# Attention output turned by a DMA in f16 halves and projected in three f16 products

## The reference, cut to what matters

```python
def _L0_xattn_ref(queries, keys, values, attn_bias, Wq, Wk, Wv, Wp):
    q = _split_heads(queries @ Wq.T, N_HEAD, D_KEY)
    k = _split_heads(keys @ Wk.T, N_HEAD, D_KEY)
    v = _split_heads(values @ Wv.T, N_HEAD, D_VALUE)
    scores = jnp.einsum('bhqd,bhkd->bhqk', q, k) * D_MODEL ** (-0.5) + attn_bias
    weights = jax.nn.softmax(scores, axis=-1)
    out = jnp.einsum('bhqk,bhkd->bhqd', weights, v)
    ...
    return out @ Wp.T

x = x + _L0_xattn_ref(_layernorm(x), ctx_1024, ctx_1024, bias, Wq, Wk, Wv, Wp)
x = x + _L0_ffn_ref(_layernorm(x), ...)   # 8 experts, each takes its top tokens
```

## Time and profile before

| What | Value |
|---|---|
| median of the runs | 1128.0 us |
| the profiled execution's own time | 1129.07 us |
| its span | 1127.3 us |
| PE busy | 1066.8 us, 95% |
| DVE busy | 888.7 us, 79% |
| ACT busy | 810.8 us, 72% |
| POOL busy | 683.3 us, 61% |
| attention stage | to about 791 us of the span |

### The profile page before, as it was taken

The page is one execution under the profiler, slowest core; times in us unless marked ns, Lnnn a source line. Parts: engine busy times, 40 slices in busy tenths (PEclk is TensorE's granted clock), DMA queues, the critical chain, the costliest instruction groups (busy, mean ns, idle before and its releaser), DMA issues. The chain is left out here.

```text
span 1127.3 us, 46562 instructions
## 1 busy us (share of the span) xinstructions
PE 1066.8 (95%) x13640; PEld 868.2 (77%) x13640; DVE 888.7 (79%) x3847; ACT 810.8 (72%) x2407; POOL 683.3 (61%) x1155
## 2 busy tenths in 40 slices
PE   4999999999999999999999999998499999999995
PEld 3888888888888888888888888886256666666664
DVE  4898898898988988989989889887765656565553
ACT  4777778777877787787778777875366666667562
POOL 5566566565665665655656656654047767767673
PEclk9999999999999999999999999999589999999998
DMA  3765555555555555555555555555001121111112
GB/s 102 121 106 109 109 100 114 105 106 111 106 103 114 100 109 107 101 114 106 105 112 105 104 113 100 111 102 86 0 11 29 29 58 37 37 56 29 50 54 66
DMA packets 307337, 96.83 MB, mean 86 GB/s; under 512 B 284256, under 2 KB 300640, under 8 KB 307296
## 3 DMA queue, kind: packets, MB, share of 16 engines
q1 hardware_dynamic: 306432, 94.16, 41.7%
q10 hardware_dynamic: 864, 2.16, 0.5%
HBM read 16.58 MB, written 4.19 MB: 18 GB/s over the span
## 5 line engine op out<-in xcount | busy, mean ns | idle before, releaser
L408 ACT ACTIVATE probs<-neg,negmax 128x120 f32<-128x120 f32 x1024 | 320.3, 383 | 157.7 <-DVE negmax L430 157.6
L430 DVE CUSTOM_DVE_ANT_0 neg<-bk_s,bias_sb 128x120 f32<-128x120 f32 x1024 | 227.5, 277 | 77.3 <-PE bk_s L550 73.7
L270 POOL CAST p_parts<-probs 128x480 f16<-128x480 f32 x256 | 150.2, 587 | 135.6 <-ACT probs L408 131.8
L1098 POOL TENSOR_TENSOR hid<-hid_f,hid 128x512 f16<-128x512 f32 x128 | 167.7, 1314 | 73.9 <-ACT hid L1052 72.9
L550 PE MATMUL bk_s<-qk 64*128 64x120 f32 x2048 | 181.4, 296 | 0.5 <-DVE negmax L430 0.5
L498 DVE TENSOR_TENSOR p_parts<-probs,p_parts 128x480 f16<-128x480 f32 x256 | 177.6, 694 | 0.7 <-POOL p_parts L270 0.5
L550 PEld LDWEIGHTS bk_s<-qk 64*128 64x128 f32 x2048 | 134.2, 186 | 45.4 <-issue 45.3
L589 PE MATMUL bk_y<-wp_sb,oT 128*128 128x128 f32 x1024 | 156.3, 275 | 0.0
L1152 DVE TENSOR_TENSOR hid_f<-bk_u,silu 128x512 f32<-128x512 f32 x128 | 88.3, 690 | 85.3 <-ACT silu L1045 35.0
L378 ACT COPY qk<-bk_a 128x496 f32<-128x496 f32 x256 | 144.7, 565 | 3.3 <-PE bk_a L537 3.3
L589 PEld LDWEIGHTS bk_y<-wp_sb,oT 128*128 128x128 f32 x1024 | 134.5, 191 | 0.2 <-ACT oT L371 0.2
(11 more groups left out here) (161 smaller groups left out, 3399.9 us busy)
## 6 DMA issues: line engine op xcount, KB each, us to landing
y_all<-y SPq DMA_DIRECT2D x128, 64.0 KB, 2.0
wst<-ffn_w SPq DMA_DIRECT2D x64, 96.0 KB, 2.3
x_sb<-x SPq DMA_DIRECT2D x64, 64.0 KB, 2.0
pT<-p_parts SPq DMA_TRANSPOSE x256, 3.1
out<-x_sb SPq DMA_DIRECT2D x16, 256.0 KB, 2.0
ctx_f<-ctx_t SPq DMA_DIRECT2D x64, 60.0 KB, 1.9
w_f<-wqkv_t ACTq DMA_DIRECT2D x3, 512.0 KB, 5.4
wp_sb<-wp_t ACTq DMA_DIRECT2D x1, 512.0 KB, 6.2
```

The costliest lines, as they stand in the source:

```text
L270: pool.tensor_copy(p_parts[g][:, 0, :, 0:K], probs[g % 2][:, :, :]).then_inc(p_hi_ready, 1)
L408: e = nc.scalar.activation(probs[g % 2][:, i, :], neg[g % 2][:, i, :], ACT.Exp, bias=negmax[g % 2][:, i:i + 1], scale=-1.0)
L430: r = nc.vector.tensor_tensor_reduce(out=neg[g % 2][:, i, :], in0=bk_s[i % 2][:, (i // 2) * K:(i // 2 + 1) * K], in1=bias_sb[:, :], scale= ...
L1098: nc.gpsimd.tensor_tensor(hid[1][par][:, ic, :], hid_f[ic % 2][:, :], hid[0][par][:, ic, :], ALU.subtract).then_inc(hid_lo_ready, 1)
```

## The change

1. PE no longer turns O. ACT writes the upper f16 half of `o_sb` (`o_parts`), POOL the lower half, and SP issues a second DMA transpose per group, 128 x 512 f16, into `oT`, right behind the turn of the probabilities in its list (`turn_o(t, g)`: group n-5, behind `turn` of group n).
2. The projection reads `oT` and `wp_hi`, `wp_lo` (made once, times 16) in six f16 products per group in place of two f32 ones. It is now for group n-8 (`PROJ_LAG` 8, before 6), and stands before PV in PE's step.
3. V has two PSUM banks (the bank of `bk_x` is free), and V stands before projection and PV, Q and K come last.
4. In DVE's step `rsum` now stands ahead of `v_lo`; the addition of the projection to x moves from step 1 to step 3 of the slot; POOL's and ACT's lists are moved to fit. `pT` and `oT` lie in the space of `w_f`.

```diff
-TURN_LAG = PV_LAG + 1
-PROJ_LAG = PV_LAG + 2
+SPLIT_LAG = PV_LAG + 1
+PROJ_LAG = PV_LAG + 4
+X1_GROUP = (PROJ_LAG + 3) % 4
...
+        pT = [turned(2 * GH * i, 2 * GH) for i in range(GROUPS)]
+        oT = [turned(2 * GH * GROUPS + 2 * GP * i, 2 * GP) for i in range(GROUPS)]
+        o_parts = [sb(f"o_parts{i}", [S, 2, GH, DH], F16) for i in range(GROUPS)]
...
-        bk_a, bk_b, bk_o, bk_x, bk_y, bk_m = (bank(n) for n in ("bk_a", "bk_b", "bk_o", "bk_x", "bk_y", "bk_m"))
+        bk_b = [bank("bk_b0"), bank("bk_b1")]
+        bk_a, bk_o, bk_y, bk_m = (bank(n) for n in ("bk_a", "bk_o", "bk_y", "bk_m"))
...
+            def turn_o(t, g):
+                b5, g5 = behind(t, g, SPLIT_LAG)
+                if live(b5):
+                    n = 4 * b5 + g5
+                    sp.wait_ge(o_lo_ready, n + 1)
+                    alone(sp)
+                    if some(n - GROUPS + 1):
+                        sp.wait_ge(proj_written, n - GROUPS + 1)
+                    alone(sp)
+                    sp.dma_start_transpose(oT[g5][:, :, :], o_parts[g5][:, :, :, :].rearrange("p a b c -> p (a b c)")
+                                           ).then_inc(oT_moved[g5], 16)
             def slot(t, par):
...
+                for g in range(GROUPS):
+                    if live(t - 1):
+                        turn(t, g)
+                    turn_o(t, g)
+                    if g == 0 and live(t + 2):
+                        load_x(t + 2, par)
+                    if g == 1 and live(t + 1):
+                        load_ffn(t + 1, (par + 1) % 2)
...
+            def lower_o(t, g):
+                b5, g5 = behind(t, g, SPLIT_LAG)
+                if live(b5):
+                    pool.wait_ge(o_hi_ready, n + 1)
+                    pool.tensor_tensor(o_parts[g5][:, 1, :, :], o_sb[g5 % 2][:, :, :], o_parts[g5][:, 0, :, :],
+                                       ALU.subtract).then_inc(o_lo_ready, 1)
...
-                    act.wait_ge(oT_written, 4 * b4 + g4 + 1)
-                    nc.scalar.copy(oT[g4 % 2][:, :, :].rearrange("p a b -> p (a b)"),
-                                   bk_x[:, 0:GP * S]).then_inc(oT_ready, 1)
+                    act.wait_ge(o_ready, 4 * b5 + g5 + 1)
+                    nc.scalar.copy(o_parts[g5][:, 0, :, :], o_sb[g5 % 2][:, :, :]).then_inc(o_hi_ready, 1)
...
-                    for j in range(GP):
-                        m = nc.tensor.transpose(bk_x[:, j * S:(j + 1) * S],
-                                                o_sb[g3 % 2][:, 2 * j:2 * j + 2, :].rearrange("p a b -> p (a b)"),
-                                                ident[:, :])
...
-                        m = nc.tensor.matmul(bk_y[:, 0:D], oT[g4 % 2][:, j, :], wp_sb[:, GP * g4 + j, :],
-                                             start=(g4 == 0 and j == 0), stop=(g4 == GROUPS - 1 and j == GP - 1))
+                    pe.wait_ge(oT_moved[g4], 16 * (b4 + 1))
+                    for j in range(GP):
+                        at = GP * g4 + j
+                        oh, ol = oT[g4][:, j, :], oT[g4][:, GP + j, :]
+                        nc.tensor.matmul(bk_y[:, 0:D], oh, wp_hi[:, at, :], start=(g4 == 0 and j == 0), stop=False)
+                        nc.tensor.matmul(bk_y[:, 0:D], oh, wp_lo[:, at, :], start=False, stop=False)
+                        m = nc.tensor.matmul(bk_y[:, 0:D], ol, wp_hi[:, at, :], start=False,
+                                             stop=(g4 == GROUPS - 1 and j == GP - 1))
```

More of the change, by code:

```diff
@@ L378, in step @@
                     nc.scalar.copy(qk[pw][:, gw, :], bk_a[:, 0:QK]).then_inc(qk_ready, 1)
[L380 to L384, removed]
+                b5, g5 = behind(t, g, SPLIT_LAG)
+                if live(b5):
+                    act.wait_ge(o_ready, 4 * b5 + g5 + 1)
+                    if some(b5):
+                        act.wait_ge(oT_moved[g5], 16 * b5)
+                    alone(act)
+                    nc.scalar.copy(o_parts[g5][:, 0, :, :], o_sb[g5 % 2][:, :, :]).then_inc(o_hi_ready, 1)
                 if gw == 2:
@@ L422, in step @@
                 tw, gw, pw = (t, g - 1, par) if g else (t - 1, GROUPS - 1, (par + 1) % 2)
+                if g == 0 and live(t + 1):
+                    dve.wait_ge(loaded_xc, (t + 2) * 32)
+                    if some(t + 1):
+                        dve.wait_ge(stats_ready, t + 1)
+                    alone(dve)
+                    nc.vector.bn_stats(stats[:, 0, :], x_sb[:, t + 1, :]).then_inc(x_stats_ready, 1)
                 if live(t - 1):
@@ L461, in step @@
-                if live(b2):
-                    dve.wait_ge(rsum_ready, 4 * b2 + g2 + 1)
-                    if some(4 * b2 + g2 - 1):
-                        dve.wait_ge(oT_written, 4 * b2 + g2 - 1)
-                    nc.vector.scalar_tensor_tensor(
-                        out=o_sb[g2 % 2][:, :, :], in0=o[:, :, 0:DH], scalar=1.0 / WSCALE,
-                        in1=rsum[:, :].rearrange("p (a b) -> p a b", b=1).to_broadcast([S, GH, DH]),
-                        op0=ALU.mult, op1=ALU.mult).then_inc(o_ready, 1)
@@ new lines, in step @@
+                if g == X1_GROUP and live(t - 3):
+                    dve.wait_ge(proj_written, 4 * (t - 3) + 4)
+                    nc.vector.scalar_tensor_tensor(
+                        out=x_sb[:, t - 3, :], in0=bk_y[:, 0:D], scalar=1.0 / (WSCALE * WSCALE),
+                        in1=x_sb[:, t - 3, :], op0=ALU.mult, op1=ALU.add).then_inc(x1_ready, 1)
+                b4, g4 = behind(t, g, PV_LAG)
+                o = bk_o[:, 0:GH * OW].rearrange("p (a b) -> p a b", a=GH)
+                if live(b4):
+                    dve.wait_ge(pv_written, 4 * b4 + g4 + 1)
+                    if some(4 * b4 + g4):
+                        dve.wait_ge(o_ready, 4 * b4 + g4)
+                    nc.vector.reciprocal(rsum[:, :], o[:, :, DH]).then_inc(rsum_ready, 1)
@@ new lines, in step @@
+                if live(tw):
+                    dve.wait_ge(v_hi_ready, 4 * tw + gw + 1)
+                    at = slice(GH * gw, GH * (gw + 1))
+                    nc.vector.tensor_tensor(v_lo[pw][0:K, at, :],
+                                            bk_b[gw % 2][0:K, 0:GH * DH].rearrange("p (a b) -> p a b", a=GH),
+                                            v_hi[pw][0:K, at, 0:DH], ALU.subtract).then_inc(v_lo_ready, 1)
+                if live(b4):
+                    dve.wait_ge(rsum_ready, 4 * b4 + g4 + 1)
+                    if some(4 * b4 + g4 - 1):
+                        dve.wait_ge(o_lo_ready, 4 * b4 + g4 - 1)
+                    nc.vector.tensor_tensor(o_sb[g4 % 2][:, :, :], o[:, :, 0:DH],
+                                            rsum[:, :].rearrange("p (a b) -> p a b", b=1).to_broadcast([S, GH, DH]),
+                                            ALU.mult).then_inc(o_ready, 1)
```

154 lines of the change are left out of this document (67 added, 87 removed).

## The result

The changed kernel takes 1323.24 us (median of four runs, 1322.11 to 1327.25), the kernel before 1128.67 on the same chip: ratio 1.1727, 95% interval 1.1697 to 1.1756. The profiled execution took 1327.25 with a span of 1325.1. The forecast was 1219, range 1155 to 1280: right in direction, less than half in size, and the time lies outside the range.

A forecast was written before the change was run, and what follows sets the result against it. A loop through projection, PV, DVE, SP and O's DMA landing was taken to bound slots at 13.3 us. 79.5 (56 slots) + 8 (unrolled) + 3 (start, end) gave +90.5 us: 1219 us, range 1155 to 1280.

The forecast's parts named there:

- the prediction's own sign: On SP's queue: SP's own time was the bound if SP has no wait for p_lo left.
- y: SP's time held by O's 512-column transpose: 0.79 us, bounds 0.33 and 1.23; SP's slot is 9.25 + 4y, 12.4 us.
- O lands 3.75 us after P's issue: Landing of O's transpose, queued behind P's on the DMA engines; bounds 3.42 and 3.96 us.
- The loop sum of 6.40 and half of the 0.5: Projection, PV, DVE, SP and landing of O: 6.40 us per two steps, plus 0.5 a slot for extra DVE work.
- B: Theory that the loop of O's landing, projection, PV, DVE and SP's issues binds, twice a slot; the prediction's loop gave 13.3 us.
- The bound as the larger of list and loop: A slot's time: the loop's 13.3 us was taken to decide, above SP's list of 12.4 us.
- the chain of steps 0 and 2: The loop's other chain, with SP's loads ahead of group 1's turn: some 0.6 us late, about the same 13.3 a slot.
- The sum: Whole kernel: 79.5 us from 56 loop slots, 8 from eight unrolled slots, 3 for start and end; +90.5 us, 1219.
- SP's own time decides: Rival on SP's queue: a half-width transpose holds SP as long as a whole one, slot 14.2 us, 1268 us; 13%.
- O lands like a plain load: Rival on O's landing: 1.9 us after its issue, slot 12.6 us, 1180 us; 9%.
- PE's relief comes through: Rival: O lands within some 2.55 us of P's issue, DVE bounds at 10.9 us a slot, 1068 us; 11%.
- TensorE's clock falls: Rival on PE: new pauses of 0.7 us a step lower its clock; with half of it, over 1600 us; 2%.

The follow-up runs named there:

- widths: Kernel before plus ten DMA transposes (128 to 2048 columns) and two plain copies on SP behind the attention loop, each waiting for the last; ran once, 1155.21 us.
- no_loads: Changed kernel without the loop's loads: later x comes in one transfer at the start, ctx and ffn_w not at all; 1284.3 us, slots 14.01.
- unread: Changed kernel whose projection reads weight blocks and doesn't wait for the turned O, which is still turned; 1254.2 us, slots 13.92.
- o_first: Changed kernel with O's transpose, on SP, moved ahead of that of the probabilities, one step earlier; 1253.21 us, slots 13.87.
- proj_late: Changed kernel with only PE's projection moved behind PV; 1268.74 us, slots 14.00.
- plain_copy: Changed kernel with a plain DMA copy of 128 x 512 in place of O's transpose, all waits kept; 1221.57 us, slots 13.13.
- no_turn: Changed kernel with no transpose of O; the projection reads weight blocks and waits for no DMA, halves of O still made; 1067.53 us, slots 10.88.
- plain_late_loads: Changed kernel with O copied instead of transposed, projection behind PV, and x, ctx, ffn_w loads on ScalarE's queue from the fifth batch; 1162.23 us, slots 12.23.
- pairs_loads_late: Changed kernel: one O transpose per two groups, ahead of P's; loads on ScalarE's queue; projection behind Q and K, x1 addition behind o_sb; 1121.22 us.
- after_loads: Changed kernel with the loads of x, ctx and ffn_w issued on ScalarE's queue from the fifth batch on; 1323.77 us, slots 14.72.

## Where the prediction was right and where it was wrong

- *PE relieved and idle, the projection waiting for O, DVE for PV, SP's spare time gone:* right. PE's wait for O is 233 us, above the 150 to 200 forecast, DVE's for PV 189. PE is busy 76% in the window, near the 80% forecast. By the prediction's own sign SP alone isn't the bound: it still waits for p_lo, 1.2 us in a slot.
- *POOL and ACT hide under the path:* right; POOL's subtraction was taken as 0.73 and takes 0.67.
- *y, SP's time for a transpose of half the width, 0.79:* wrong, 1.19. This is the first of two steps that failed. I took the plain load's 0.33 plus half of the rest, because most of a transpose's price "likely goes with its size"; widths shows that next to none of it does. The upper bound, 1.23, was the nearest row: the same instruction. With 1.19 the list is 14.0 and no longer hides under 13.3: 0.7 us a slot. Alone this step doesn't explain the miss: the prediction's own sum with y at 1.23 gives 1268, still 55 us short.
- *O lands 3.75 us after P's issue:* 3.9 (1.4 to 1.6 to its issue, 2.45 from there), near the upper bound of 3.96.
- *The loop sum of 6.40 and half of the 0.5, 6.65 a round:* measured by no_loads as 7.30 and 6.69. Some 0.3 of the 0.7 is O's landing over a slot's two rounds, 0.4 p_lo beside POOL, which the prediction priced at 0.2 twice a slot and left out of its sum. B alone is 14.0, not 13.3. (For that price it compared p_lo's 0.86 beside POOL's cast with 0.65 "with POOL otherwise engaged"; in that 0.65, at 407.86, POOL was idle.)
- *The bound as the larger of list and loop:* wrong, and the second step that failed, worth the other 0.8 us a slot. The prediction saw the loads only as a delay in the chain of steps 0 and 2, some 0.6 late, "which brings it to about the same 13.3". In fact a stretch of full list (9.55 us) and a round's tail (5.3 us) make one chain of 14.85, longer than the list alone (13.9 to 14.0 in unread, o_first and proj_late) and the loop alone (14.0 in no_loads). The same y is in that stretch: P's issue to the next one across the loads is 3.15 + y, 4.33 measured (503.26 to 507.59) and 3.9 in the working. No rival named a chain through both.
- *The sum:* counted by the x1 additions, one a batch, 63 slots of after are 189 us longer than those of before; the working had 87.5. Some 1.5 us in each of 56 slots is 84, what the third to seventh slots take above the later ones another 8; the rest is in the other unrolled slots. Start and end are some 9 us longer, against 3.
- *Rival "SP's own time decides", 14.2 a slot, 1268:* its condition held (the half width holds SP as long as the whole), and unread, o_first and proj_late, where the list is what is left, come out at 1253 to 1269. Its 13% rested on the same wrong argument as y. But even with its condition true the changed kernel isn't that case: it takes 1323.
- *Rival "O lands like a plain load", 1180:* it didn't happen, O lands 2.45 after its issue. With a real copy, which lands in 2.0, the kernel takes 1222 (plain_copy).
- *Rival "PE's relief comes through", 1068:* it didn't happen, but its price was right: no_turn is 1067.5 with slots of 10.88 (10.9 in the working), with DVE as the bound.
- *Rival "TensorE's clock falls":* the grant is 0.97 from 100 to 500 us with the new pauses, and lower only in the first slots. It doesn't make the 14.8: the chain above has only 0.9 us of PE in it (515.30 to 516.21).
- *The rule that transposing DMAs are as fast as regular ones* (the Trainium skill, Advanced Engine Details and Errata, X-Bar Transpose (TRN2)) does not hold for the transposes here: 1.19 against 0.57 us of SP and 2.4 against 2.0 to landing, at 512 columns.

Still open: how the loads lengthen a landing (that they do shows in every slot, the mechanism doesn't), what bounds plain_late_loads at 12.2, and what bounds pairs_loads_late.

## What to carry to other kernels

Count the time that transposes hold a queue by instructions, not by bytes: where the trace has one row of the same instruction, its duration is the estimate and a smaller operand is no reason for a smaller price; then merge what can be merged. When two resources each fill almost the whole period, ask for a chain that goes through both before taking the larger. A wait put ahead of independent work in an in-order list costs the round trip of whatever it waits for, and moving the cause to another queue can turn issue time into landing time: move it also to a moment when nothing urgent is in flight.

## What was not expected of the hardware

- A DMA transpose holds SP for 1.135, 1.182, 1.192, 1.232 and 1.317 us at 128, 256, 512, 1024 and 2048 columns; a copy within SBUF 0.57 and 0.48 us at 512 and 1024.
- Transfers that overlap from two queues land later: in after_loads O's turn beside the loads 3.6 us after its issue on average (3.12 to 4.31) instead of 2.4, x 3.0 instead of 1.8.
- The clock granted to PE was 0.83 on average in 60 to 100 us of after and 0.97 from 100 to 500, with PE busy 76% of the time in both; what brought it down there these rows don't tell.
